# A decoder layer with routed experts: the first layer of half tiles in plain float32, and high and low weights side by side in the second layer

## The chip, the core and the metric

The kernel runs on one core of a Trainium2 chip. Its time is the device time of one execution in microseconds. Five engines work side by side, each through its own list of instructions, and meet at semaphores: TensorE (matrix products, PE in the profile), VectorE (DVE), ScalarE (ACT), GpSimd (POOL) and SyncE (SP), which here does nothing but start transfers. A product has a standing operand, which is loaded first (PEld), and a moving one, whose columns stream past it. Results land in eight banks of 512 float32 columns.

## What is computed

A pre-norm decoder layer on 2048 tokens of width 256: linear attention with 16 heads, a cross attention, and a feed-forward layer in which each token goes to two of eight experts. The change touches only the experts:

```python
probs = softmax(einsum('bnd,ed->bne', xn, Wg))      # two experts are chosen for each token
def body(acc, params):
    w1, b1e, w2, b2e, g = params
    h = gelu(einsum('bnd,df->bnf', xn, w1) + b1e)    # 256 -> 1024
    y = einsum('bnf,fd->bnd', h, w2) + b2e           # 1024 -> 256
    return (acc + g[..., None] * y, None)
```

## The kernel before

**Tiles.** A first part computes the attentions and sorts the tokens by expert. The experts then work on 23 tiles of gathered tokens: 16 full tiles of 256 rows (F) and 7 half tiles of 128 rows (H), in the order `KIND = "FFFFF" + "FFHFFHFHFHFFHFHFHF"`. So the half tiles are 7, 10, 12, 14, 17, 19 and 21. Each tile has its own expert, whose weights (1 MB for each layer) are loaded from memory.

**High and low parts.** A product of the type float32r is rounded, so an operand is split in a high part (ScalarE copies it to float32r) and a low part (VectorE subtracts the high part from the original). Three products, high by high, high by low and low by high, then stand for one exact product. Tile 0 in its first layer (`NL = 1`) and tiles 0 to 2 in their second (`NP = 3`) use plain float32 products instead, one for three.

**A full tile.** The first layer has the weights standing and 256 token columns moving: 48 products (L964, L965, L969). The result has the hidden units on the partitions, so ScalarE's GELU takes the bias for each partition, and its high and low parts stand as operands of the second layer: for each 128 rows 24 products of 256 columns (L1020, L1021, L1022), 8 terms of three.

**A half tile.** Its first layer has the tokens standing and 512 columns of weights moving: 12 products by the helper `three` (L446). The result has tokens on the partitions. So VectorE adds the bias row (`add_bias`, L1995, from `b1r`, 512 KB that a transfer has spread over the partitions), ScalarE applies GELU to it (L1408), and eight transposes (`turn`, L989) bring it into the form of the second layer; the high and low parts are then taken from the banks (L1414, L2000).

**The order.** The lists are written out by hand. For a half tile t TensorE does its first layer, the transposes of the next tile's tokens (L453), and the second layer of tile t-1 with `turn(t)` between its two halves. For the full tile after it, it does the first layer and then the half tile's second. The second layer of a tile thus always runs a tile late. `w1r`, `w1h`, `w1l`, `w2r`, `w2h` and `w2l` have two buffers each, `xf` and `hf` have one, and the second layers write banks 5 and 6 (F) or 7 (H). SyncE starts, for each t in turn, the loads `w1(t+1)`, `w2(t)` and the biases of t (and for half tiles `b1r`). A load that waits holds up all those behind it. `w1(t+1)` waits until the low parts of w1(t-1) are made (L499), which is when its buffer is free.

Of the kernel before, what the change touches and what calls it, by code (L numbers as in the profile page):

```python
# [43 lines left out]
def decoder_layer(nc, x, ctx_in, ctxT, aw, ab, awo, xw, xfc, ff, b1, gb, wg, consts, out):  # L44
# [11 lines left out]
    with ExitStack() as top:  # L56
# [174 lines left out]
        w2h0 = sb("w2h0", [P, 2048], f32r)  # L231
        w2l0 = sb("w2l0", [P, 2048], f32r)
# [5 lines left out]
        w2h1 = sb("w2h1", [P, 2048], f32r)  # L238
        w2l1 = sb("w2l1", [P, 2048], f32r)
# [56 lines left out]
        b1r = sb("b1r", [P, F])  # L296
        w1r, w1h, w1l = [w1r0, w1r1], [w1h0, w1h1], [w1l0, w1l1]
        w2r, w2h, w2l = [w2r0, w2r1], [w2h0, w2h1], [w2l0, w2l1]
# [16 lines left out]
        d_rb = sem("d_rb")  # L315
# [24 lines left out]
        m_w1h, m_w1l, m_w2h, m_w2l, m_xp, m_xf, m_xh, m_xl, m_l1, m_hf, m_hh, m_hl, m_l2, m_ya, m_yb, m_gb, m_gx, m_hb, m_ht = (  # L340
            sem(f"m_{n}") for n in ("w1h", "w1l", "w2h", "w2l", "xp", "xf", "xh", "xl", "l1", "hf", "hh", "hl", "l2", "ya", "yb", "gb", "gx", "hb", "ht"))
# [31 lines left out]

        def parts(t):
            return 2 * (t - NL)

        def halves_of(t):
            return 2 * KIND[:t].count("H")
# [58 lines left out]

        def weigh_on_act(t):
            return t < 4
# [18 lines left out]
        def sync(e):  # L458
# [24 lines left out]
            def load_w1(t):  # L483
# [113 lines left out]
        def tensor(e):  # L597
# [330 lines left out]
            def layer1(t, q):  # L928
# [4 lines left out]
                if q == 0 and t >= NL:  # L933
                    e.wait_ge(m_w1l, parts(t) + 2)
                    e.wait_ge(m_xh, t + 1 - NL)
# [12 lines left out]
                if t >= 2 and KIND[t - 1] == "H":  # L948
                    if q < 2:
                        e.wait_ge(m_hb, halves_of(t - 1) + q + 1)  # L950
                    else:
                        e.wait_ge(m_hl, split(t - 1) + q - 1)
# [3 lines left out]
                for m in range(2):  # L956
# [9 lines left out]
                    if q == 0 and m == 0:  # L966
                        e.wait_ge(m_xl, t + 1 - NL)
# [5 lines left out]
            def layer1_half(t, q):  # L973
                k = t % 2
                if q == 0:
                    e.wait_ge(m_w1l, parts(t) + 2)
                    e.wait_ge(m_xl, t + 1 - NL)
                e.wait_ge(m_hf, 8 * (t - 1) + 2 * q + 2)
                c = slice(q * 512, q * 512 + 512)
                three(e, banks[q][:, :], lambda j: xh[k][:, j, 0:128], lambda j: xl[k][:, j, 0:128],  # L980
                      lambda j: w1h[k][:, :].rearrange("p (j n) -> p j n", j=2)[:, j, c],
                      lambda j: w1l[k][:, :].rearrange("p (j n) -> p j n", j=2)[:, j, c], 2, True).then_inc(m_l1, 2)

            def turn(t):
                h = fl(hf)
                for c in range(2):
                    e.wait_ge(m_hf, 8 * t + 4 * c + 4)
                    for j in range(4):
                        last = e.transpose(banks[2 + c][:, j * 128:j * 128 + 128],  # L989
                                           h[:, c * 512 + j * 128:c * 512 + j * 128 + 128], ident)  # L990
                    last.then_inc(m_ht, 1)

            def layer2(t, i, terms=range(8)):
# [20 lines left out]
                w_low = w2l[k][:, :].rearrange("p (j n) -> p j n", j=8)  # L1014
                for j in terms:
# [65 lines left out]
            for t in range(5, NT):  # L1081
                if KIND[t] == "H":
# [4 lines left out]
                    turn(t)  # L1087
# [29 lines left out]
        def scalar(e):  # L1117
# [228 lines left out]
            def x_affine(t):  # L1346
# [3 lines left out]
                if t > NL:  # L1350
                    e.wait_ge(m_xl, t - NL)
# [20 lines left out]
            def gelu(t, q):  # L1372
# [13 lines left out]
                if q == 0 and t >= 1 and KIND[t - 1] == "H":  # L1386
                    e.wait_ge(m_ht, halves_of(t))
# [22 lines left out]
            def turned_high(t, c):  # L1410
                e.wait_ge(m_ht, halves_of(t) + c + 1)
                if c == 0:
                    e.wait_ge(m_l2, BEFORE[t - 1])
                e.activation(hh[t % 2][:, 4 * c:4 * c + 4, 0:128], banks[2 + c][:, :].rearrange("p (j n) -> p j n", j=4),  # L1414
                             ACT.Copy).then_inc(m_hh, 1)
# [66 lines left out]
            for t in range(5, NT):  # L1482
                if KIND[t] == "H":
# [7 lines left out]
                    turned_high(t, 0)  # L1491
                    turned_high(t, 1)
# [3 lines left out]
                if t + 1 < NT:  # L1496
# [9 lines left out]
                if t == 5 or (KIND[t - 1] == "H" and t + 1 < NT):  # L1506
                    x_affine(t + 1)
                gelu(t, 1)
                if t == NT - 1:
# [1031 lines left out]
```

## Times and profile before

| | |
|---|---|
| median of three runs | 404.87 us (402.98 to 405.08) |
| profiled execution, whole | 402.5 us |
| its span on the core | 400.7 us |
| TensorE busy | 390.9 us, 98% |
| VectorE busy | 340.6 us, 85% |
| ScalarE busy | 307.2 us, 77% |
| GpSimd busy | 238.7 us, 60% |
| TensorE's granted clock | 0.999 of full |

The span is the part of the execution from the first to the last instruction. A product's busy time holds its whole way through the array, and neighbours overlap; so what a product costs in a stream is read from the distance between starts, not from its duration. The same holds, less strongly, of ScalarE and VectorE.

### The profile page before, as it was taken

How to read it: one execution, taken by the hardware profiler on the slowest of the kernel's cores; microseconds unless marked ns; L12 is line 12 of the kernel's file. 1: busy time of each engine (PE TensorE's matmuls, PEld its weight loads, DVE VectorE, ACT ScalarE, POOL GpSimd, SP SyncE). 2: the span in 40 equal slices, each digit the busy share in tenths (PEclk: the TensorE clock that was granted, in tenths of full speed). 3: DMA queues.
4: the chain of work that ended last, by engine and by line, in shares of the span. 5: the costliest groups of instructions: out<-in, count | busy, mean ns of one | idle time of the engine just before them, and what ended most of it. 6: DMA issues, size and time to landing. Idle time of an engine off the chain costs nothing.

```text
span 400.7 us, 8846 instructions
## 1 busy us (share of the span) xinstructions
PE 390.9 (98%) x2953; PEld 372.4 (93%) x2953; DVE 340.6 (85%) x847; ACT 307.2 (77%) x621; POOL 238.7 (60%) x353
## 2 busy tenths in 40 slices
PE   7999999999999999999999999999999999999994
PEld 7789899999989999899999999999999999999994
DVE  5697788888889878899685999979999988999972
ACT  5577777686776769346999988988988988989770
POOL 3546476757667666878873765546656373645443
PEclk9999999999999999999999999999999999999999
DMA  7920031220102742678599798996989897899633
GB/s 256 349 98 29 1 103 48 66 80 27 56 28 65 269 142 96 212 281 265 155 384 295 224 334 262 288 319 216 375 269 345 267 314 266 259 335 315 152 37 39
DMA packets 32738, 79.33 MB, mean 198 GB/s; under 512 B 4691, under 2 KB 24021, under 8 KB 26806
## 3 DMA queue, kind: packets, MB, share of 16 engines
q1 hardware_dynamic: 23728, 67.68, 48.1%
q0 software_dynamic: 7488, 10.39, 12.4%
q10 hardware_dynamic: 1478, 0.72, 0.7%
q8 instruction: 23, 0.38, 0.4%
q14 instruction: 21, 0.17, 0.1%
HBM read 69.14 MB, written 9.63 MB: 197 GB/s over the span
## 4 chain that ended last, share of the span: by engine, by line
PE 91%; DVE 4%; POOL 1%; issue 1%; DMA 1%; ACT 1%; ACTq 0%; DVEq 0%
PE bank L446 21%; PE bank L1020 8%; PE bank L1021 8%; PE bank L1022 8%; PE bank L964 7%; PE bank L969 7%; PE bank L965 7%; PE bank L453 6%; PE bank L1008 3%; PE bank L961 2%; PE bank L816 2%; PE bank L768 2%; PE bank L989 2%; PE bank L683 1%; PE bank L798 1%
## 5 line engine op out<-in xcount | busy, mean ns | idle before, releaser
L2425 POOL DMA_INDIRECT y_<-yb,idxs x29 | 55.3, 1906 | 68.6 <-DMA y_<-yb,idxs 42.3
L1020 PE MATMUL bank<-w2h,hh 128*128 128x256 f32 x264 | 75.4, 286 | 0.0
L1021 PE MATMUL bank<-w2l,hh 128*128 128x256 f32 x264 | 74.1, 281 | 0.0
L1022 PE MATMUL bank<-w2h,hl 128*128 128x256 f32 x264 | 74.1, 281 | 0.0
L964 PE MATMUL bank<-xh,w1h 128*128 128x256 f32 x240 | 64.3, 290 | 0.0
L965 PE MATMUL bank<-xh,w1l 128*128 128x256 f32 x240 | 62.6, 282 | 0.0
L2369 POOL DMA_INDIRECT xg<-xn_rows,idxg x39 | 48.9, 1254 | 15.6 <-issue 11.3
L1702 DVE TENSOR_TENSOR w1l<-w1r,w1h 128x1024 fp32r<-128x1024 f32 x44 | 53.7, 1221 | 2.0 <-ACT w1h L1131 1.7
L1978 DVE TENSOR_TENSOR w2l<-w2r,w2h 128x1024 fp32r<-128x1024 f32 x40 | 48.6, 1218 | 2.5 <-ACT w2h L1138 2.5
L1021 PEld LDWEIGHTS bank<-w2l,hh 128*128 128x128 f32 x264 | 50.0, 189 | 0.0
L1020 PEld LDWEIGHTS bank<-w2h,hh 128*128 128x128 f32 x264 | 50.0, 189 | 0.0
L1022 PEld LDWEIGHTS bank<-w2h,hl 128*128 128x128 f32 x264 | 49.9, 189 | 0.0
L1138 ACT ACTIVATE w2h<-w2r 128x1024 fp32r<-128x1024 f32 x40 | 41.1, 1055 | 10.7 <-PE bank L1022 8.6
L969 PE MATMUL bank<-xl,w1h 128*128 128x256 f32 x240 | 48.3, 283 | 0.0
L1390 ACT ACTIVATE hf<-bank,bs 128x256 f32<-128x256 f32 x104 | 42.1, 477 | 5.5 <-PE bank L969 4.9
L1131 ACT ACTIVATE w1h<-w1r 128x1024 fp32r<-128x1024 f32 x44 | 44.5, 1052 | 2.3 <-DMA w1r<-ff_ 2.3
L965 PEld LDWEIGHTS bank<-xh,w1l 128*128 128x128 f32 x240 | 45.8, 191 | 0.1
L964 PEld LDWEIGHTS bank<-xh,w1h 128*128 128x128 f32 x240 | 45.8, 191 | 0.1
L969 PEld LDWEIGHTS bank<-xl,w1h 128*128 128x128 f32 x240 | 37.3, 191 | 0.0
L1354 ACT ACTIVATE xf<-bank,gbT 128x256 f32<-128x256 f32 (+1 forms) x46 | 21.9, 529 | 12.0 <-PE bank L453 8.3
L2007 DVE TENSOR_TENSOR hl<-hf,hh 128x1024 fp32r<-128x1024 f32 x25 | 30.1, 1223 | 0.6 <-issue 0.6
L2425 POOL DMA_INDIRECT y_<-yb,idxg x10 | 20.5, 2053 | 15.2 <-ACT yb L1370 6.8
(309 smaller groups left out, 1103.3 us busy)
## 6 DMA issues: line engine op xcount, KB each, us to landing
w1r<-ff_ SPq DMA_DIRECT2D x23, 1024.0 KB
w2r<-ff_ SPq DMA_DIRECT2D x23, 1024.0 KB
b1r<-b_ SPq DMA_DIRECT2D x7, 512.0 KB
bs<-ff_ SPq DMA_DIRECT2D x23, 132.0 KB
xn_rows<-xn SPq DMA_DIRECT2D x8, 264.0 KB, 2.2
xin<-x_ SPq DMA_DIRECT2D x8, 256.0 KB, 7.0
cT<-ctxT_ SPq DMA_DIRECT2D x8, 256.0 KB, 4.5
cin<-ctx_ SPq DMA_DIRECT2D x8, 256.0 KB, 3.2
```

The lines of the kernel that those rows point to most:

```text
L446: r = e.matmul(o, a_(t), b_(t), start=first and m == 0, stop=m == n - 1)
L964: e.matmul(o, w_high[:, j, c], xh[k][:, j, :], start=j == 0, stop=False)
L965: e.matmul(o, w_low[:, j, c], xh[k][:, j, :], start=False, stop=False)
L969: last = e.matmul(o, w_high[:, j, c], xl[k][:, j, :], start=False, stop=j == 1)
L1020: e.matmul(bank_y(t, i)[:, 0:D], hh[k][:, j, c], w_high[:, j, :], start=j == 0, stop=False)
L1021: e.matmul(bank_y(t, i)[:, 0:D], hh[k][:, j, c], w_low[:, j, :], start=False, stop=False)
L1022: last = e.matmul(bank_y(t, i)[:, 0:D], hl[k][:, j, c], w_high[:, j, :], start=False, stop=j == 7)
L1131: e.activation(w1h[k][:, s], w1r[k][:, s], ACT.Copy).then_inc(m_w1h, 1)
L1702: e.tensor_tensor(w1l[k][:, s], w1r[k][:, s], w1h[k][:, s].bitcast(fp32), ALU.subtract).then_inc(m_w1l, 1)
L1978: e.tensor_tensor(w2l[k][:, s], w2r[k][:, s], w2h[k][:, s].bitcast(fp32), ALU.subtract).then_inc(m_w2l, 1)
L2369: e.indirect_dma_start(out=xg[k][:, i, :], out_offset=None, in_=xn_d[0:ready, :], in_offset=bass.IndirectOffsetOnAxis(ap=idxg[:, COL[t] + ...
L2425: e.indirect_dma_start(out=out[:, :], out_offset=bass.IndirectOffsetOnAxis(ap=at, axis=0), in_=yb[t % 2][:, i, :], in_offset=None, compute ...
```

## The change

There are two edits. Half tiles: the first layer becomes 16 plain float32 products with the original weights standing and 128 token columns moving; its weights and tokens are no longer split, `add_bias`, `turn` and the load of `b1r` are gone, and GELU takes the bias for each partition in eight operations of 128 columns. Second layers of tiles 3 to 20: high and low weights lie side by side in one tensor `w2s`, so that one product of 512 columns gives high by high in columns 0 to 255 of the bank and high by low in columns 256 to 511; the third product is as before. VectorE then adds the two halves with one operation more for each 128 rows (30 of these).

```diff
@@ load_w1
-                if t >= NL + 2:
+                if t >= NL + 2 and KIND[t - 2] == "F":
                     e.wait_ge(m_w1l, parts(t - 1))
+                if t >= NL + 2 and KIND[t - 2] == "H":
+                    e.wait_ge(m_l1, 4 * (t - 1))
@@ load_b
-                if KIND[t] == "H":
-
-                    if halves_of(t):
-                        e.wait_ge(m_hb, halves_of(t))
-                    else:
-                        e.wait_ge(p_lg, NB)
-                    e.dma_start(b1r[:, :], b1[bass.ds(regs[t], 1), :].to_broadcast([P, F])).then_inc(d_rb, 16)
@@ layer1_half
                 if q == 0:
-                    e.wait_ge(m_w1l, parts(t) + 2)
-                    e.wait_ge(m_xl, t + 1 - NL)
+                    e.wait_ge(d_w1[k], 16 * (t // 2 + 1))
+                    e.wait_ge(m_xf, 2 * t + 2)
                 e.wait_ge(m_hf, 8 * (t - 1) + 2 * q + 2)
-                c = slice(q * 512, q * 512 + 512)
-                three(e, banks[q][:, :], ...).then_inc(m_l1, 2)
-
-            def turn(t):
-                ...
+                w_plain = w1r[k][:, :].rearrange("p (j n) -> p j n", j=2)
+                for m in range(4):
+                    c = slice((4 * q + m) * 128, (4 * q + m + 1) * 128)
+                    for j in range(2):
+                        last = e.matmul(banks[q][:, m * 128:(m + 1) * 128], w_plain[:, j, c], xf[:, j, 0:128],
+                                        start=j == 0, stop=j == 1)
+                last.then_inc(m_l1, 2)
@@ layer2
+                    if side_by_side(t):
+                        if j == 7:
+                            e.matmul(bank_y(t, i)[:, 0:D], hl[k][:, j, c], w_high[:, j, :], start=False, stop=False)
+                        last = e.matmul(bank_y(t, i)[:, :].rearrange("p (s n) -> p s n", s=2), hh[k][:, j, c], w_both[:, :, j, :],
+                                        start=j == 0, stop=j == 7)
+                        if j < 7:
+                            e.matmul(bank_y(t, i)[:, 0:D], hl[k][:, j, c], w_high[:, j, :], start=False, stop=False)
+                        continue
@@ scalar
             def x_affine(t):
-                if t > NL:
-                    e.wait_ge(m_xl, t - NL)
+                if t > NL and KIND[t - 1] == "F":
+                    e.wait_ge(m_xl, splits(t))
+                if t > NL and KIND[t - 1] == "H":
+                    e.wait_ge(m_l1, 4 * t)
@@
             def gelu_half(t, c):
-                e.wait_ge(m_hb, halves_of(t) + c + 1)
-                h = fl(hf)[:, c * 512:c * 512 + 512]
-                e.activation(h, h, ACT.Gelu_apprx_tanh).then_inc(m_hf, 4)
+                e.wait_ge(m_l1, 4 * t + 2 * c + 2)
+                e.wait_ge(m_hl, split(t - 1) + c + 1)
+                ...
+                for m in range(4):
+                    j = 4 * c + m
+                    e.activation(hf[:, j, 0:128], banks[c][:, m * 128:(m + 1) * 128], ACT.Gelu_apprx_tanh,
+                                 bias=bs_[t % 3][:, j:j + 1]).then_inc(m_hf, 1)
@@ the full tile behind a half one: the high parts of the next w1 come after gelu(t, 1)
+                after = KIND[t - 1] == "H" and t + 1 < NT
-                if t + 1 < NT:
+                if not after and t + 1 < NT and KIND[t + 1] == "F":
                     w1_high(t + 1, 0)
                     w1_high(t + 1, 1)
...
                 gelu(t, 1)
+                if after and KIND[t + 1] == "F":
+                    w1_high(t + 1, 0)
+                    w1_high(t + 1, 1)
@@ vector, weigh
+                if side_by_side(t):
+                    e.tensor_tensor(ya[:, i, :], bank_y(t, i)[:, D:2 * D], bs_[t % 3][:, 8:8 + D], ALU.add).then_inc(m_yl, 1)
+                    e.wait_ge(m_yl, n - BEFORE[NP] + 1)
+                    e.tensor_tensor(ya[:, i, :], bank_y(t, i)[:, 0:D], ya[:, i, :], ALU.add).then_inc(m_ya, 1)
```

Here `side_by_side(t)` is `NP <= t < NT - 2`. `add_bias` leaves VectorE's list; its splits of w1 and x are made for full tiles alone; behind a half tile it makes the low parts of w2 before those of the next w1.

On TensorE, at half tile 12, the list before begins its first layer so (`w1h`, `w1l`: high and low weights; `xh`, `xl`: tokens), and further down has the transposes of `turn`:

```order
L446 MATMUL bank<-w1h,xh 128x512 [waits m_hf,m_xl,m_w1l]
L446 MATMUL bank<-w1l,xh 128x512
L446 MATMUL bank<-w1h,xl 128x512
L446 MATMUL bank<-w1h,xh 128x512
```

```order
L989 MATMUL bank<-cs,hf 128x128 [waits m_hf]
L989 MATMUL bank<-cs,hf 128x128 x3
```

The changed list has for both the rows below (`w1r`: the weights as loaded, `xf`: the tokens), and behind them the second layer of the tile before in pairs of a 512 and a 256 column product (`w2s`: both parts of the weights):

```order
L975 MATMUL bank<-xf,w1r 128x128 [waits m_hf,m_xf,d_w11]
L975 MATMUL bank<-xf,w1r 128x128 x7
L975 MATMUL bank<-xf,w1r 128x128 [waits m_hf]
L975 MATMUL bank<-xf,w1r 128x128 x7
```

```order
L1010 MATMUL bank<-w2s,hh 128x512 [waits m_hl,m_ya,m_w2l]
L1013 MATMUL bank<-w2s,hl 128x256
L1010 MATMUL bank<-w2s,hh 128x512
L1013 MATMUL bank<-w2s,hl 128x256
```

The half tile's first layer no longer waits for splits but for the loaded weights and the scaled tokens, and its transposes are gone.

SyncE's list before, for t of a half tile and the full tile behind it (`w1r` and `w2r` are 1 MB loads):

```order
L512 ISA [waits m_hb]
L512 DMA b1r<-b1_ 128x1024
L499 TENSOR_LOAD tei [waits m_w1l]
L499 ISA x2
L500 ISA
L500 DMA w1r0<-ff_ 128x2048
L526 ISA [waits m_w2l]
L526 DMA w2r1<-ff_ 128x2048
```

And changed:

```order
L501 TENSOR_LOAD tei [waits m_l1]
L501 ISA x2
L502 ISA
L502 DMA w1r0<-ff_ 128x2048
L521 ISA [waits m_w2l]
L521 DMA w2r1<-ff_ 128x2048
```

The load of `w1r` for the second tile behind a half tile now waits for the half tile's first layer on TensorE (`m_l1`) and no longer for VectorE's low parts (`m_w1l`), and the `w2r` of the tile between stands behind it.

## Rows read from the trace of the kernel before

**Rows 1.** Page, part 1: busy time, share and instructions of each engine.

```profile
PE 390.9 (98%) x2953; PEld 372.4 (93%) x2953; DVE 340.6 (85%) x847; ACT 307.2 (77%) x621; POOL 238.7 (60%) x353
```

**Rows 2.** Page, part 4: shares of the chain that ended last, by engine.

```profile
PE 91%; DVE 4%; POOL 1%; issue 1%; DMA 1%; ACT 1%; ACTq 0%; DVEq 0%
```

**Rows 3.** Waits of TensorE, the two longest: total us, times, longest.

```profile
PE bank L864 <- POOL xnT L2191: 1.4, 1, 1.4
PE bank L625 <- DVE aw_l L1586: 1.0, 1, 1.0
```

**Rows 4.** Busy time in stretches: half and full tile 12, 13; then 14 to 16.

```profile
core 0: us, PE busy (x) PEld busy (x) DVE busy (x) ACT busy (x) POOL busy (x), PEclk, DMA share, GB/s
...
284.94:303.48 18.54, 18.54 (x148) 18.00 (x147) 18.03 (x29) 16.69 (x26) 11.99 (x7) 1.00 0.95 320
303.48:333.90 30.42, 30.42 (x248) 29.87 (x247) 27.06 (x44) 26.52 (x42) 16.31 (x11) 1.00 0.93 306
```

**Rows 5.** TensorE in time at half tile 12: start us, busy us, operation.

```profile
284.78 0.40 PE L446 MATMUL bank<-w1h,xh 128*128 128x512 f32 x1
...
287.53 0.60 PE L453 MATMUL bank<-cs,xg 128*128 128x128 f32 x4
...
290.80 1.03 PE L989 MATMUL bank<-cs,hf 128*128 128x128 f32 x8
291.59 0.36 PE L1020 MATMUL bank<-w2h,hh 128*128 128x256 f32 x1
291.79 0.28 PE L1021 MATMUL bank<-w2l,hh 128*128 128x256 f32 x1
...
294.50 0.28 PE L964 MATMUL bank<-xh,w1h 128*128 128x256 f32 x1
```

**Rows 6.** TensorE in time at its plain float32 products.

```profile
100.61 1.05 PE L768 MATMUL bank<-va,phk 128*128 128x129 f32 x8
101.50 0.96 PE L683 MATMUL bank<-wg_f,xnT 128*128 128x8 f32 x8
...
150.62 3.62 PE L961 MATMUL bank<-xf,w1r 128*128 128x256 f32 x16
154.07 0.60 PE L453 MATMUL bank<-cs,qsb 128*128 128x128 f32 x4
```

**Rows 7.** VectorE in time at half tile 12.

```profile
286.06 0.41 DVE L2053 TENSOR_TENSOR ya<-bank,bs 128x256 f32<-128x256 f32 x1
286.51 0.35 DVE L2060 TENSOR_SCALAR yb<-ya,small 128x256 f32<-128x256 f32 x1
...
288.34 1.22 DVE L1702 TENSOR_TENSOR w1l<-w1r,w1h 128x1024 fp32r<-128x1024 f32 x1
289.47 1.22 DVE L1978 TENSOR_TENSOR w2l<-w2r,w2h 128x1024 fp32r<-128x1024 f32 x1
```

**Rows 8.** ScalarE in time at tiles 12 and 13; in brackets idle time before and its end.

```profile
285.04 1.06 ACT L1138 ACTIVATE w2h<-w2r 128x1024 fp32r<-128x1024 f32 x1 [0.75 <-PE bank L1022]
286.01 1.99 ACT L1131 ACTIVATE w1h<-w1r 128x1024 fp32r<-128x1024 f32 x2
287.90 1.25 ACT L1408 ACTIVATE hf<-hf 128x512 f32<-128x512 f32 x2
289.05 1.00 ACT L1354 ACTIVATE xf<-bank,gbT 128x256 f32<-128x256 f32 x2
...
297.79 0.81 ACT L1354 ACTIVATE xf<-bank,gbT 128x128 f32<-128x128 f32 x2 [0.30 <-issue]
298.49 1.57 ACT L1390 ACTIVATE hf<-bank,bs 128x256 f32<-128x256 f32 x4
```

**Rows 9.** SyncE in time: the issues of 1 MB loads around half tile 14.

```profile
301.11 0.33 SPq L500 DMA_DIRECT2D w1r<-ff_  x1
302.32 0.33 SPq L526 DMA_DIRECT2D w2r<-ff_  x1
```

**Rows 10.** Transfers from 284 to 304 us in 40 slices: GB/s moved.

```profile
GB/s 473 387 475 410 393 410 361 426 410 442 317 215 272 255 235 206 36 21 0 213 180 344 426 426 410 426 311 229 410 426 336 207 258 425 418 428 448 281 361 369
```

More of the change, by code:

```diff
@@ L41, with decoder_layer @@
 NCONST = _at
-def decoder_layer(nc, x, ctx_in, ctxT, aw, ab, awo, xw, xfc, ff, b1, gb, wg, consts, out):
+def decoder_layer(nc, x, ctx_in, ctxT, aw, ab, awo, xw, xfc, ff, gb, wg, consts, out):
     fp32 = mybir.dt.float32
@@ L295, in decoder_layer @@
         yb1 = sb("yb1", [P, 2, D])
-        b1r = sb("b1r", [P, F])
         w1r, w1h, w1l = [w1r0, w1r1], [w1h0, w1h1], [w1l0, w1l1]
-        w2r, w2h, w2l = [w2r0, w2r1], [w2h0, w2h1], [w2l0, w2l1]
+        w2r, w2s = [w2r0, w2r1], [w2s0, w2s1]
+        w2h, w2l = [w[:, 0, :] for w in w2s], [w[:, 1, :] for w in w2s]
         hp = [hp0, hp1]
@@ L372, in split, with splits @@
             return 2 * (t - NP)
+        def splits(t):
+            return KIND[NL:t].count("F")
         def parts(t):
-            return 2 * (t - NL)
-        def halves_of(t):
-            return 2 * KIND[:t].count("H")
+            return 2 * splits(t)
         def ry(t, name):
@@ L436, in high_on_act, with side_by_side @@
             return t < NE
+        def side_by_side(t):
+            return NP <= t < NT - 2
         def weigh_on_act(t):
@@ L934, in layer1 @@
                     e.wait_ge(m_w1l, parts(t) + 2)
-                    e.wait_ge(m_xh, t + 1 - NL)
+                    e.wait_ge(m_xh, splits(t) + 1)
                 if t == 0 and q == 2:
@@ L947, in layer1 @@
                     e.wait_ge(m_hf, 8 * (t - 1) + 2 * q + 2)
[L948 to L952, printed above, removed]
+                if t >= 2 and KIND[t - 1] == "H" and q < 2:
+                    e.wait_ge(m_hf, 8 * (t - 1) + 4 * q + 4)
                 w_plain = w1r[k][:, :].rearrange("p (j n) -> p j n", j=2)
@@ L966, in layer1 @@
                     if q == 0 and m == 0:
-                        e.wait_ge(m_xl, t + 1 - NL)
+                        e.wait_ge(m_xl, splits(t) + 1)
                     for j in range(2):
@@ L1505, in scalar @@
                     weigh(3, 1)
-                if t == 5 or (KIND[t - 1] == "H" and t + 1 < NT):
+                if t == 5 or after:
                     x_affine(t + 1)
                 gelu(t, 1)
+                if after and KIND[t + 1] == "F":
+                    w1_high(t + 1, 0)
+                    w1_high(t + 1, 1)
                 if t == NT - 1:
@@ L1986, in x_split, with half_low @@
                     e.tensor_copy(xh[k][:, :, 0:n], xf[:, :, 0:n]).then_inc(m_xh, 1)
-                e.wait_ge(m_xh, t + 1 - NL)
+                e.wait_ge(m_xh, splits(t) + 1)
                 e.tensor_tensor(xl[k][:, :, 0:n], xf[:, :, 0:n], xh[k][:, :, 0:n].bitcast(fp32), ALU.subtract).then_inc(m_xl, 1)
-            def add_bias(t, c):
-                e.wait_ge(m_l1, 4 * t + 2 * c + 2)
-                e.wait_ge(d_rb, 8 * halves_of(t) + 16)
-                e.wait_ge(m_hl, split(t) - 1)
-                s = slice(c * 512, c * 512 + 512)
-                e.tensor_tensor(fl(hf)[:, s], banks[c][:, :], b1r[:, s], ALU.add).then_inc(m_hb, 1)
-            def turned_low(t, c):
+            def half_low(t, c):
                 e.wait_ge(m_hh, split(t) + c + 1)
                 s = slice(4 * c, 4 * c + 4)
-                e.tensor_tensor(hl[t % 2][:, s, 0:128], banks[2 + c][:, :].rearrange("p (j n) -> p j n", j=4),
+                e.tensor_tensor(hl[t % 2][:, s, 0:128], hf[:, s, 0:128],
                                 hh[t % 2][:, s, 0:128].bitcast(fp32), ALU.subtract).then_inc(m_hl, 1)
@@ L2052, in weigh @@
                     e.wait_ge(m_yb, BEFORE[t - 1] + i + 1)
-                e.tensor_tensor(ya[:, i, :], bank_y(t, i)[:, 0:D], bs_[t % 3][:, 8:8 + D], ALU.add).then_inc(m_ya, 1)
+                if side_by_side(t):
+                    e.tensor_tensor(ya[:, i, :], bank_y(t, i)[:, D:2 * D], bs_[t % 3][:, 8:8 + D], ALU.add).then_inc(m_yl, 1)
+                    e.wait_ge(m_yl, n - BEFORE[NP] + 1)
+                    e.tensor_tensor(ya[:, i, :], bank_y(t, i)[:, 0:D], ya[:, i, :], ALU.add).then_inc(m_ya, 1)
+                else:
+                    e.tensor_tensor(ya[:, i, :], bank_y(t, i)[:, 0:D], bs_[t % 3][:, 8:8 + D], ALU.add).then_inc(m_ya, 1)
                 if weigh_on_act(t):
@@ L2132, in vector @@
                     w2_low(t, 1)
-                    turned_low(t, 0)
-                    turned_low(t, 1)
+                    half_low(t, 0)
+                    half_low(t, 1)
                     weigh(t - 1, 1)
                 elif KIND[t - 1] == "H":
-                    if t + 1 < NT:
+                    w2_low(t, 0)
+                    w2_low(t, 1)
+                    if t + 1 < NT and KIND[t + 1] == "F":
                         w1_low(t + 1, 0)
-                    w2_low(t, 0)
-                    if t + 1 < NT:
                         w1_low(t + 1, 1)
                         x_split(t + 1)
-                    w2_low(t, 1)
                     if t == NT - 1:
@@ L2155, in vector @@
                 else:
-                    w1_low(t + 1, 0)
-                    x_split(t + 1)
-                    w1_low(t + 1, 1)
+                    if KIND[t + 1] == "F":
+                        w1_low(t + 1, 0)
+                        x_split(t + 1)
+                        w1_low(t + 1, 1)
                     w2_low(t, 0)
```

43 lines of the change are left out of this document (13 added, 30 removed).

## The prediction

> **What bounds the kernel now.** I read the busy times first. TensorE is busy 390.9 of 400.7 us [rows 1]; the others are not near it over the whole span. The chain of work that ended last says the same, 91% of it on TensorE [rows 2], and TensorE's list of waits is almost empty: the two longest are single waits of 1.4 and 1.0 us at the start, far from the experts [rows 3]. In the expert part the reader should see two things in the table by stretch [rows 4]: for a half tile and the full tile behind it (18.54 us) TensorE has no gap, and the others are not far behind: VectorE 18.03, ScalarE 16.69, transfers 0.95 of the time. So time taken from TensorE counts one to one, but only a couple of microseconds for each pair of tiles before something else is late. The working therefore has two steps: what TensorE loses, and whether the others follow.
>
> **Half tiles, first layer.** What goes: 12 products of 512 columns, from 284.78 to 287.53 [rows 5], 2.75 us or 0.229 each, and the eight transposes of `turn`, from 290.80 to the next product at 291.59, plus the 0.08 by which the first product behind them is stretched (0.20 to its successor where 0.12 is normal) [rows 5], 0.87 us. Together 3.62. What comes: 16 plain float32 products with 128 columns moving and new weights each. The nearest row is the plain product of 129 columns, eight from 100.61 to 101.50, 0.111 each [rows 6]; half of a 256 column one would be 0.108 (16 from 150.62 to 154.07 are 0.216 each [rows 6]), and 0.116 would take in some slack. I take 0.111: 1.78 us (1.73 to 1.86). The switch to plain products and back was there before (the transposes of the next tile follow in both), so it costs nothing more. Gain 1.84 us for each half tile, 12.9 us for seven.
>
> The row of the 256 column plain product shows 0.216 us, about two passes of 256 columns at the full clock of 2.4 GHz. The Trainium skill (FP8 and Floating Point Precision, TensorE Precision Notes) says that true float32 takes four passes through the array, which speaks against this edit. By that rule 16 products of 128 columns would be an estimated 16 x 4 x 128 / 2.4 GHz = 3.4 us, and the edit would gain only 0.2 us for each half tile; by the rows it gains 1.84. The measured row contradicts the rule at 256 columns, so I go by the row and keep the rule's outcome as a rival below.
>
> **Second layers.** 30 blocks of 128 rows (12 full tiles of two and 6 half tiles, in tiles 3 to 20), each 24 products of 256 columns. From 291.79 to 294.50 there are 23 of them [rows 5], 0.118 each, so 2.83 us for a block. Now 8 products of 512 and 8 of 256: 8 x (0.229 + 0.118) = 2.78. Gain 0.05 for a block, 1.5 us in all. A joined product saves only the small overhead between two products and one weight load, not columns. Bounds: if a product of 512 ran as tightly as plain ones do (0.216) the gain is 8 x 0.020 = 0.16 for a block, 4.7 us; if joining gave nothing, 0. That the moving operand comes in two strips 8 KB apart isn't shown anywhere in the trace; with 0.006 us for each product, the spread that I see between 512 column ones, it could be a loss of 8 x 30 x 0.006 - 1.5, about nothing. I take 1.5.
>
> So TensorE loses 12.9 + 1.5 = 14.4 us.
>
> **VectorE.** Added: 30 additions like the one at 286.06, 0.45 from start to start [rows 7], 13.5 us. Each is queued ahead of the weighing that writes the rows out, and `ya` is later by 0.45; but the bank is next written a tile later or more, so TensorE doesn't see it. Removed for each half tile: two bias additions of 512 (some 0.6 each by half the 1.13 of 1024 columns [rows 7]), two low parts of w1 (2 x 1.13), one split of x (0.7): about 4.1, for seven 29 us. Taking low parts from `hf` instead of a bank is the same size. Net 15 us lighter. For a pair half + full that is 18.0 - 4.1 + 3 x 0.45 = 15.2, against 16.5 for TensorE. The cover holds.
>
> **ScalarE.** Removed: two high parts of w1 for each half tile, 0.97 each [rows 8], 1.9. GELU: two operations of 512 that took 1.15 [rows 8] become eight of 128. Four of 256 take 1.57 - 0.1, 0.37 each; a 128 column operation is 0.1 shorter than one of 256 (0.81 against 1.00 for a pair of `xf` [rows 8]), so 0.27, and 2.2 for eight (2.9 if a short one costs as much as a long one). Net 16.7 - 1.9 + 1.0 = 15.8 us for a pair, against 16.5. It goes from 90% to 95% of the pair, the tightest of all.
>
> **The load queue.** The new wait is here. Before, w1(16) was issued at 301.11 and w2(15) at 302.32 [rows 9], 2.2 and 1.0 us before half tile 14 began on TensorE (303.32, which is 284.78 [rows 5] and 18.54 for the pair [rows 4]). Now w1 of the second tile behind a half one waits for the half tile's first layer, 1.8 us after it begins, and w2 of the tile between is queued behind it. So both come 3 to 4 us later, as 2.1 MB together. By hand, with 0 at the start of the half tile's first layer and the order of the lists: TensorE does the first layer to 1.8, transposes to 2.2, the second layer of the full tile before to 7.8, the next full tile's first layer with the short transposes to 13.7, and the half tile's second to 16.5. ScalarE, which starts on w2 of the half tile at 0 when its buffer is free, is through w1, GELU, `xf`, w2 and the high parts of h at 8.1, and wants w2 of the full tile then; it would be done at 15.8 of 16.5. `xf` is ready at 6.0, its splits on VectorE at 7.1, and TensorE wants them at 7.8. So that load may be late by some 0.75 + 0.7 = 1.4 us, land at 9.5, 7.7 after its issue, before TensorE waits. Transfers run at 410 to 430 GB/s in bursts [rows 10], 5.1 us for 2.1 MB, or 6.6 at the 320 GB/s of the pair [rows 4]; about 0.9 goes by before the first bytes move. That lands it 6 to 7.5 us after issue: just in time. The bytes themselves fall by 0.5 MB for each half tile (`b1r`).
>
> Where two full tiles follow a half one (tiles 8, 9 and 15, 16) the high parts of the next w1 now stand behind `gelu(t, 1)`, and end at about 15.5 where that load is a microsecond late; low parts and the split of x follow to 17.3 and 17.9, where TensorE wants the high part of x at 17.0: 0.3 to 0.5 us for each. I set 1.5 us for all such waits, with 0 and 6 as ends.
>
> **Sum.** 402.5 (the profiled execution, of which 400.7 is span) - 14.4 + 1.5 = 389.6. The median of the runs shown lay 2.4 above the profiled execution and the lowest 0.5 above; I add 1.4: 391.0 us.
>
> **Rivals.**
> The first: the others don't follow, and ScalarE or the load of w2 takes TensorE's place. For it: 95% load of ScalarE, and a margin of 1.4 us on a load that shares the transfer engines with gathers and scatters. Against: 0.7 us of idle time is left in each pair, and VectorE and the bytes are relieved. If short GELUs cost 0.37, ScalarE needs 16.6 of 16.5 and the chain to `xf` is 0.8 longer; if w2 lands 9 us after issue, 1.3 us are lost. At 0.7 to 1.3 us for each of seven half tiles that is 5 to 9 us: 394.5 to 398.5.
>
> The second: a plain product of 128 columns takes as long as one of 256, 0.216 us [rows 6], because a plain product would be bound by something other than its columns. Then the half tile's layer is 3.46 for 3.62, and the time is 402.5 - 7 x 0.16 - 1.5 + 1.4 = 401.3. Against it: 0.111 at 129 columns and 0.101 at 8 columns in the same trace [rows 6]. The four passes of the page named above would end in the same place.
>
> The third ends slower: w2 behind the held up w1 lands so late that each half tile loses more than the 14.4 / 7 = 2.06 us that it gains. It decides from 7.7 + 2.06 = 9.8 us after issue, 2.1 MB at under 236 GB/s after the first 0.9. Slices of 206 to 235 GB/s exist while scatters run [rows 10], but for 2 us and not for 9. At 200 GB/s the load takes 11.4, each half tile loses 3.7, and the time is 402.5 - 14.4 + 26 + 1.4, about 415; just past the point it is 406.
>
> That the change does nothing: if the pair were in truth bound by transfers (0.95 share [rows 4]), only the bytes saved would count, 0.5 of 5.9 MB, or 1.6 us for each half tile, and the time would be 402.5 - 11 + 1.4 = 393; this lies inside the first rival.
>
> **Chances and range.** Forecast, 388 to 394: 0.72. First rival, with transfers as the bound: 0.18. Second: 0.03. Third: 0.04, nearly all slower. Some smaller mix that ends within half a per cent of before: 0.03. Measured on this kernel, changes under 0.5% can't be told from none. So faster 0.93, same 0.03, slower 0.04. The range goes from 387.0 (the second layers gain 4.7, no waits) to 397.5 (most of the first rival).
>
> **What would show it.** In the changed profile: 16 plain products of a half tile in about 1.8 us with the next transposes right behind; pairs in the second layers at 0.35 us; the pair of tiles 12 and 13 in about 16.6 us and the group of three 14 to 16 in about 28.5 (30.42 before). TensorE's waits should stay under 3 us in the expert part, and be for the splits of x behind a half tile. I am wrong in the step on the load queue if ScalarE's high parts of w2 wait long for transfers, and in the step on TensorE if the 128 column plain products stand further apart than 0.12 us.

## The result: slower by 2.2%, and the profile after

The changed kernel takes 413.51 us (median of four, 410.95 to 415.2) against 404.72 for the kernel before, measured beside it: a ratio of 1.022, 95% interval 1.016 to 1.028. Some executions of either kernel run slower at a slightly lower granted clock, and all times and ratios in this document are of the others. The prediction said 391.0 (387.0 to 397.5) with a chance of 0.93 for faster. It was wrong in size and in sign.

The page of the changed kernel begins its busy times (part 1) and its chain by engine (part 4) so:

```profile
PE 392.7 (95%) x2797; PEld 364.6 (89%) x2797; DVE 325.8 (79%) x835; ACT 299.4 (73%) x649; POOL 240.4 (58%) x353
...
PE 67%; DMA 12%; DVE 10%; ACT 4%; issue 4%; POOL 1%; SPq 1%; ACTq 0%; DVEq 0%; POOLq 0%
```

Against [rows 1, 2]: VectorE and ScalarE are lighter by 15 and 8 us (15 and some 6 were worked out), but TensorE isn't lighter at all (392.7 for 390.9), its share of the span fell, and a quarter of the chain has moved away from it, 11% to transfers and 6% to VectorE. The same stretches as in [rows 4], half and full tile 12 and 13, then 14 to 16:

```profile
core 0: us, PE busy (x) PEld busy (x) DVE busy (x) ACT busy (x) POOL busy (x), PEclk, DMA share, GB/s
...
289.02:307.43 18.41, 18.41 (x136) 17.32 (x135) 15.52 (x25) 15.74 (x31) 11.68 (x8) 1.00 0.88 296
307.43:342.29 34.86, 32.09 (x219) 29.90 (x218) 27.33 (x44) 27.51 (x50) 19.58 (x12) 0.95 0.80 245
```

The pair takes 18.41 for 18.54, where 16.6 was forecast: no gap, so the work itself is not shorter. The group of three takes 34.86 for 30.42, with 2.8 us in which TensorE is idle, and a stretch at a lower clock. Measured from one half tile's first layer to the next, the other group (tiles 7 to 9) went from 30.51 to 33.97, the pair behind tile 19 from 18.62 to 19.74. These, 0.9 us before tile 7 and 1.2 at the end, less 0.6 that the three other pairs gain, are the 10.6 us between the spans (411.3 and 400.7).

**The plain first layer.** TensorE in time at half tile 14, of the changed kernel, and a block of 128 rows in a second layer:

```profile
229.63 0.40 PE L1010 MATMUL bank<-w2s,hh 128*128 128x512 f32 x1
229.87 0.28 PE L1013 MATMUL bank<-w2s,hl 128*128 128x256 f32 x1
229.99 0.39 PE L1010 MATMUL bank<-w2s,hh 128*128 128x512 f32 x1
...
232.43 0.28 PE L956 MATMUL bank<-xh,w1h 128*128 128x256 f32 x1
...
307.43 3.73 PE L975 MATMUL bank<-xf,w1r 128*128 128x128 f32 x32
310.99 0.60 PE L453 MATMUL bank<-cs,xg 128*128 128x128 f32 x4
```

The block takes 2.80 us (229.63 to 232.43; forecast 2.78, before 2.83): that term holds. The first layer takes 3.56 us, not 1.78. The spacing, 0.111, is what was forecast; but there are 32 rows for the 16 products in the code. A plain float32 product stands in the trace as two rows. The same could have been read before, and it holds for the rows at 129 and 8 columns in [rows 6] too: `keys_values` and `crossed_q` have four calls each for their eight rows. The kernel before has 16 plain products in tile 0's first layer (four parts, two blocks, two contraction halves), and its line reads:

```profile
L961 PE MATMUL bank<-xf,w1r 128*128 128x256 f32 x32 | 7.4, 379 | 0.0
```

So the 0.216 of [rows 6] is half a product; a whole one of 256 columns takes 0.43 us, 4 x 256 columns at 2.4 GHz. The rule of the Trainium skill that the prediction set aside (FP8 and Floating Point Precision, TensorE Precision Notes: four passes) agrees with the trace: the estimate by it was 3.4 us for this layer, and 3.56 was measured.

**The groups of three.** SyncE, ScalarE and TensorE of the changed kernel, from half tile 14 (begins at 307.43) to full tile 16:

```profile
311.90 0.33 SPq L502 DMA_DIRECT2D w1r<-ff_  x1
312.42 0.33 SPq L521 DMA_DIRECT2D w2r<-ff_  x1
312.93 0.33 SPq L507 DMA_DIRECT2D bs<-ff_  x1
```

```profile
316.26 1.21 ACT L1414 ACTIVATE hh<-hf 128x512 fp32r<-128x512 f32 x2
321.04 2.01 ACT L1132 ACTIVATE w2s<-w2r 128x1024 fp32r<-128x1024 f32 x2 [3.57 <-DMA w2r<-ff_]
322.95 0.82 ACT L1384 ACTIVATE hf<-bank,bs 128x256 f32<-128x256 f32 x2
323.66 1.02 ACT L1350 ACTIVATE xf<-bank,gbT 128x256 f32<-128x256 f32 x2
324.56 0.85 ACT L1384 ACTIVATE hf<-bank,bs 128x256 f32<-128x256 f32 x2
325.28 2.02 ACT L1125 ACTIVATE w1h<-w1r 128x1024 fp32r<-128x1024 f32 x2
```

```profile
326.04 0.38 PE L453 MATMUL bank<-cs,xg 128*128 128x128 f32 x2
329.19 0.36 PE L956 MATMUL bank<-xh,w1h 128*128 128x256 f32 x1 [2.77 <-DVE w1l L1705]
...
330.46 0.41 PE L956 MATMUL bank<-xh,w1h 128*128 128x256 f32 x1
330.68 0.41 PE L957 MATMUL bank<-xh,w1l 128*128 128x256 f32 x1
```

The loads go out 4.5 us after the half tile begins (1.8 was forecast, the longer first layer is in it). w2 is there 8.6 us after its issue (6 to 7.5 was forecast); ScalarE waits 3.57 us for it. The high parts of w1 (16), whose last packet came at 317.9 and which could have been made in that time, stand behind w2, two GELUs and `xf`; their low parts come at 328.8, and TensorE waits. From 330.4 to 333.0 its products stand 0.21 apart, not 0.12: the granted clock there is 0.50 of full, its lower level (1.2 GHz), and a dozen products cost 1.2 us more. In the chain, 9.84 us are the landing of the biases of tile 15, queued behind both weights:

```profile
312.93 9.84 DMA bs<-ff_
...
325.41 0.96 ACT w1h L1125
326.39 0.98 DVE w1l L1705
327.54 1.23 DVE w1l L1705
```

### The profile page after: what moved, and what is told of

It reads as the page before. It is cut to its first block, busy times and chain, and to the rows that moved or that the text cites. A ratio compares the mean times of both kernels' runs of the same rounds, so it can differ in the third digit from the quotient of the medians.

```text
span 411.3 us, 8487 instructions
## 1 busy us (share of the span) xinstructions
PE 392.7 (95%) x2797; PEld 364.6 (89%) x2797; DVE 325.8 (79%) x835; ACT 299.4 (73%) x649; POOL 240.4 (58%) x353
## 4 chain that ended last, share of the span: by engine, by line
PE 67%; DMA 12%; DVE 10%; ACT 4%; issue 4%; POOL 1%; SPq 1%; ACTq 0%; DVEq 0%; POOLq 0%
PE bank L446 15%; PE bank L1010 7%; DMA bs<-ff_ 7%; PE bank L961 5%; PE bank L956 5%; PE bank L453 5%; PE bank L957 5%; PE bank L975 3%; PE bank L994 3%; PE bank L1013 3%; DMA w2r<-ff_ 2%; DMA y_<-yb,idxs 2%; DVE w1l L1705 2%; PE bank L953 2%; PE bank L811 2%
## 5 line engine op out<-in xcount | busy, mean ns | idle before, releaser
L1010 PE MATMUL bank<-w2s,hh 128*128 128x512 f32 x240 | 86.4, 398 | 0.0
L1132 ACT ACTIVATE w2s<-w2r 128x1024 fp32r<-128x1024 f32 x40 | 41.6, 1068 | 29.4 <-DMA w2r<-ff_ 26.6
L1013 PE MATMUL bank<-w2s,hl 128*128 128x256 f32 x210 | 58.9, 280 | 0.0
L2368 POOL DMA_INDIRECT xg<-xn_rows,idxg x39 | 47.5, 1219 | 16.1 <-issue 10.6
L1981 DVE TENSOR_TENSOR w2s<-w2r,w2s 128x1024 fp32r<-128x1024 f32 x40 | 48.2, 1220 | 10.2 <-ACT w2s L1132 10.2
L1010 PEld LDWEIGHTS bank<-w2s,hh 128*128 128x128 f32 x240 | 44.7, 188 | 8.0
L1384 ACT ACTIVATE hf<-bank,bs 128x256 f32<-128x256 f32 x104 | 42.8, 485 | 10.6 <-PE bank L961 8.8
L1705 DVE TENSOR_TENSOR w1l<-w1r,w1h 128x1024 fp32r<-128x1024 f32 x30 | 36.4, 1221 | 8.4 <-ACT w1h L1125 8.1
L1013 PEld LDWEIGHTS bank<-w2s,hl 128*128 128x128 f32 x210 | 39.6, 188 | 0.3
L1125 ACT ACTIVATE w1h<-w1r 128x1024 fp32r<-128x1024 f32 x30 | 30.5, 1051 | 2.7 <-DMA w1r<-ff_ 2.7
L2424 POOL DMA_INDIRECT y_<-yb,idxg x10 | 19.4, 1940 | 15.8 <-ACT yb L1366 6.4
L1392 ACT ACTIVATE hh<-hf 128x1024 fp32r<-128x1024 f32 x25 | 26.8, 1073 | 0.4
L975 PEld LDWEIGHTS bank<-xf,w1r 128*128 128x128 f32 x224 | 26.0, 192 | 0.4
```

Of the source, the lines that this page charges most:

```text
L1010: last = e.matmul(bank_y(t, i)[:, :].rearrange("p (s n) -> p s n", s=2), hh[k][:, j, c], w_both[:, :, j, :], start=j == 0, stop=j == 7)
L1013: e.matmul(bank_y(t, i)[:, 0:D], hl[k][:, j, c], w_high[:, j, :], start=False, stop=False)
L1132: e.activation(w2h[k][:, s], w2r[k][:, s], ACT.Copy).then_inc(m_w2h, 1)
L1384: e.activation(hidden(t, j), banks[bank1(t, q)][:, m * 256:(m + 1) * 256], ACT.Gelu_apprx_tanh, bias=bs_[t % 3][:, j:j + 1]).then_inc(m_hf, 1)
L1705: e.tensor_tensor(w1l[k][:, s], w1r[k][:, s], w1h[k][:, s].bitcast(fp32), ALU.subtract).then_inc(m_w1l, 1)
L1981: e.tensor_tensor(w2l[k][:, s], w2r[k][:, s], w2h[k][:, s].bitcast(fp32), ALU.subtract).then_inc(m_w2l, 1)
```

## The experiments

Times are medians. Ratios are to the kernel before, measured beside each group of runs, with 95% intervals.

**Each edit alone.** `e1` puts the side by side second layers into the kernel before (its edit is that of the change in `layer2` and `weigh`). `e2` takes them out of the changed one:

```diff
         def side_by_side(t):
-            return NP <= t < NT - 2
+            return False
```

> The kernel before with the side by side second layers alone (tiles 3 to 20); half tiles as before. Theory A (the plain first layer gives TensorE nothing, and the load queue behind it loses the time): this edit is harmless and worth the 1.5 us of overhead in 240 joined products, so about 403.2 us (ratio 0.996), no new waits on TensorE. Theory B (the 30 added additions on VectorE, at 18.0 of 18.5 us in a pair of tiles, delay the low parts): slower than before by 3 us or more, with waits of TensorE for w1l or hl.

> The changed kernel with the three products of before in all second layers and no added additions; so the half tile edit alone. Theory A: the whole loss stays and the 1.5 us of the other edit is missing: 413 to 416 us, TensorE waits for w1l in the two groups half, full, full. Theory B: most of the loss goes, about 404.

e1: 407.88 us, 1.012 (1.004 to 1.020). e2: 409.81 us, 1.013 (1.007 to 1.020). Both edits lose alone. For e1 theory A was wrong and theory B right; the stretches of tiles 10, 11 and of 12, 13 show why:

```profile
core 0: us, PE busy (x) PEld busy (x) DVE busy (x) ACT busy (x) POOL busy (x), PEclk, DMA share, GB/s
265.60:284.50 18.90, 18.90 (x124) 16.79 (x122) 18.59 (x30) 16.57 (x26) 9.80 (x6) 1.00 0.86 265
284.50:304.10 19.60, 19.27 (x124) 16.87 (x123) 19.25 (x32) 16.57 (x26) 9.19 (x6) 1.00 0.93 307
```

VectorE had 18.03 of 18.54 us [rows 4]; three more additions of 0.45 make 19.4, and with 19.25 it is the bound of the second pair. In the changed kernel the half tiles' edit makes room for them (15.52), so the two losses are not to be added: e1's does not occur there. In e2 the pairs are as in the changed kernel (18.49) and the groups about as long (32.63 and 35.48 for 33.97 and 34.86): the loss of the groups belongs to the half tiles' edit.

**The order of the loads, and the cost that was forecast.** `e3` issues w2 and the biases first; `e4` leaves out one contraction half:

```diff
@@ e3
-                if t + 1 < NT:
+                behind = KIND[t - 1] == "H"
+                if t + 1 < NT and not behind:
                     load_w1(t + 1)
                 load_w2(t)
                 load_b(t)
+                if t + 1 < NT and behind:
+                    load_w1(t + 1)
@@ e4, layer1_half
-                    for j in range(2):
+                    for j in range(1):
```

> The changed kernel, but for the full tile behind a half tile SyncE issues w2 and the biases of that tile ahead of w1 of the next tile, so that only this w1 waits for the half tile's first layer. Theory A: ScalarE's wait for w2 (26.6 us in all) goes, so do TensorE's waits of 1.9 and 2.8 us for w1l in the groups half, full, full and the stretch at a low clock behind the second: 402 to 405 us. Rival C (the loss in these groups is made by ScalarE's new order, high parts of w1 behind the second GELU, and not by the loads): still 410 or more.

> The changed kernel with only one of the two contraction halves in the half tiles' plain first layer (8 products for 16, the sum over the other 128 inputs is left out), so that this layer costs TensorE the 1.8 us that was forecast. If the product's cost was the only step that failed, the time falls by 12.5 us below before, to some 391. Theory A (the load queue fails too, whatever the product costs): the loads are issued 1.8 us earlier and are wanted 1.8 us earlier, so the groups half, full, full still lose 3 us each and the pairs begin to lose too: 398 to 403 us.

e3: 406.76 us, 1.004 (1.000 to 1.008); 7 us better than the changed kernel, less than expected. e4: 403.90 us, 1.000 (0.996 to 1.004). In e4 two of the four pairs take the forecast 16.6 us (16.61, 16.55; the others 17.61 and 18.13), but the groups take 35.91 and 34.09, 70.0 us together where the changed kernel has 68.8, though each has 1.8 us less work: TensorE waits 7.0 us for w1l. So the loads fail whatever the product costs. In e3 the wait for w1l is gone, and the first group takes 31.29 us; the second still takes 34.43, with another wait in its place:

```profile
PE bank L453 <- DMA xg<-xn_rows,idxg: 3.6, 4, 2.5
```

These are the gathered tokens of a later tile, which GpSimd issues behind scatters.

**Loads that are never held up.** In `e6` a half tile's w1 goes to its own high or low buffer, unused there, so `w1r` is free as early as before, and that load is issued behind w2 and the biases; w1 is split ahead of w2 again. `e7` is e6 without side by side, `e8` is e6 with one contraction half. `e9` is the kernel before with the new wait added:

```diff
@@ e6, load_w1 (and its own semaphores for half tiles)
-                if t >= NL + 2 and KIND[t - 2] == "F":
+                if t >= NL + 2 and KIND[t] == "F":
                     e.wait_ge(m_w1l, parts(t - 1))
-                if t >= NL + 2 and KIND[t - 2] == "H":
-                    e.wait_ge(m_l1, 4 * (t - 1))
+                if t >= NL + 2 and KIND[t] == "H":
+                    e.wait_ge(m_l1, 4 * (t - 1 if KIND[t - 2] == "F" else t - 3))
@@ e9, load_w1 of the kernel before
+                if t >= NL + 2 and KIND[t - 2] == "H":
+                    e.wait_ge(m_l1, 4 * (t - 1))
```

> The changed kernel (both edits), but a half tile's w1 is loaded into its high or low buffer, which it doesn't use, so that no load waits for a half tile's first layer, and ScalarE and VectorE split the next w1 first, as before. Queue theory: the held up loads are the whole loss, since VectorE is lighter by the half tiles' edit; TensorE then has its 1.5 + 0.35 us back: 401.5 us (ratio 0.995 to 1.0), groups of tiles 7 to 9 and 14 to 16 at 30.2 us. Rival (the longer way to yb and GpSimd's chain of scatters, gathers queued behind them, also loses): 405 or more, with TensorE waiting for gathers.

> As the kernel before in this call, without side by side second layers and their additions. Queue theory: 403, 1.5 us more than with them. Rival: faster than with them, since each weighing is 0.45 us shorter.

> The kernel with free loads and only one of the two contraction halves in the half tiles' plain first layer (the other half of that sum is left out), so the cost that was forecast, 1.8 us, with loads as early as before. If these two steps are all that failed, the time is the forecast's, 388 to 392 us, pairs at 16.6 us and groups of three at 28.4. If ScalarE, transfers or GpSimd's chain can't follow, 393 to 400.

> The kernel before with one wait added: w1 of the second tile behind a half tile is issued only after the half tile's first layer. Nothing else changes. Queue theory: this wait alone costs most of what the change lost, 6 to 10 us, in every pair and group since ScalarE splits w1 first here. Rival (before had 5 us of slack on these loads): no change.

| | us | ratio | 95% |
|---|---|---|---|
| e6 | 404.03 | 1.000 | 0.997 to 1.003 |
| e7 | 404.55 | 1.004 | 1.001 to 1.007 |
| e8 | 404.06 | 1.000 | 0.998 to 1.003 |
| e9 | 404.26 | 1.002 | 1.000 to 1.004 |

e6 brings the time back to that of before. It undoes two things at once, the held up loads and ScalarE's new order, which are taken apart below. It stays above the expected 401.5: its groups take 31.1 us each, and TensorE waits 2.1 us for gathers. e7 is not told apart from it, so no gain or loss of the side by side products is shown here. The same wait in the kernel before costs almost nothing (e9, groups 31.08 and 30.87 for 30.51 and 30.41), which theory had not foreseen. And e8 stayed far from 388 to 392: with the cost of the product and the loads both mended, something else holds it at 404. TensorE's longest waits there are for gathered tokens, and the chain of e8 from 260 to 330 us consists of scatters:

```profile
PE bank L471 <- DMA xg<-xn_rows,idxg: 7.2, 3, 2.9
```

```profile
by line: DMA y_<-yb,idxs 86.7%; POOL y_ L2444 11.2%; issue 9.4%; POOLq L2442 0.2%
...
275.10 2.08 POOL y_ L2444
277.18 0.30 issue
277.49 6.97 DMA y_<-yb,idxs
...
285.25 1.94 POOL y_ L2444
287.19 0.30 issue
287.50 6.93 DMA y_<-yb,idxs
```

GpSimd adds each tile's rows into the output and must not begin before the tile before has landed, since a token can stand in both. A full tile costs two issues and a landing of 7 us, 10 us in all, a half one 7.7: 17.7 us for a pair, where TensorE needs 18.5 in the kernel before and 16.6 here. GpSimd itself is busy 58% of the time.

**Two chains of scatters.** Here odd tiles are added into a second buffer and each scatter waits for the tile two before it:

```diff
-                if t >= 1 and i == 0:
-                    e.wait_ge(d_s, 16 * BEFORE[t])
+                if t >= 2 and i == 0:
+                    e.wait_ge(*scattered(t - 2))
...
-                    out=out[:, :], out_offset=bass...
+                    out=(out_odd if t % 2 else out)[:, :], out_offset=bass...
```

> The kernel before, but tiles take turns between two chains of scatters: odd tiles are added into a second buffer in memory (so their part is missing in the output), and a scatter waits for the landing of the tile two before it, not of the last one. Chain theory (the loop of scatter, landing, next scatter on GpSimd needs as long for a tile as TensorE does, 9.2 us, and is a second bound beside it): TensorE bounds here anyway, so no more than 1 to 3 us less in the expert part, plus some 6 us at the end, where the last scatters no longer wait for each other: 396 to 402. Rival (the chain has slack): only the end changes.

> The changed kernel with the same two chains. If the held up loads alone make its loss in the groups of three, these still take 34 us and the time stays 8 us above the two chain version of before. If the chain of scatters takes part (late yb, gathers late behind it), the groups shrink and the gap too.

> The kernel with free loads and a half tile's first layer at the cost that was forecast (one contraction half left out), with two chains of scatters (odd tiles missing in the output). Chain theory: the chain was what held it at 404; now pairs of tiles take 16.6 us and groups of three 28.5, and the time is 12 to 13 us under the two chain version of before: 384 to 388. Rival (ScalarE or the weights' transfers bound it): within 4 us of it.

> Both edits as they are, with free loads, with two chains of scatters (odd tiles missing in the output). Chain theory: TensorE's saving of 1.5 to 1.9 us shows: that much under the two chain version of before, pairs at 18.4 and groups of three at 30.1 us. Rival: no different from it.

| with two chains | us | ratio | 95% |
|---|---|---|---|
| e10, before | 402.60 | 0.997 | 0.995 to 0.999 |
| e11, changed | 415.34 | 1.027 | 1.019 to 1.036 |
| e12, free loads, forecast cost | 392.61 | 0.970 | 0.964 to 0.977 |
| e13, free loads | 400.93 | 0.992 | 0.989 to 0.995 |

e12 against e8: 11.5 us, so the single chain was what hid the forecast. Its stretches (tiles 12, 13 and 14 to 16), and those of e13:

```profile
280.30:296.90 16.60, 16.60 (x119) 15.54 (x118) 15.45 (x25) 15.18 (x30) 9.60 (x7) 1.00 0.97 311
296.90:326.30 29.40, 29.15 (x204) 26.71 (x203) 26.06 (x43) 25.51 (x47) 18.56 (x11) 1.00 0.88 282
```

```profile
284.20:302.60 18.40, 18.40 (x136) 17.32 (x135) 15.50 (x26) 15.65 (x30) 12.41 (x7) 1.00 0.91 290
302.60:332.70 30.10, 30.10 (x219) 28.32 (x218) 25.61 (x43) 25.15 (x46) 16.87 (x9) 1.00 0.82 255
```

16.60 is the forecast's 16.6, and 392.6 is near its 391.0: the arithmetic on TensorE, VectorE (15.45 for 15.2) and ScalarE (15.18 for 15.8) was sound for a first layer of that cost. The 384 to 388 expected of e12 was too low: it is 10.0 us under e10 and not 12 to 13, its second group takes 29.4 us, and the end did not shorten. e13 against e10 is 1.7 us, TensorE's saving of 1.5 + 0.35. e11 against e13 is 14.4 us, the price of the held up loads together with the new order. The groups of e11 are still 36.19 and 34.15 us, so the chain of scatters did not make the changed kernel's loss; why e11 lies 12.7 us above e10, where 8 was expected, is open. In e10 the end of the run did not shorten by the 6 us that I had expected of it.

**The load or the order.** `e14` is the changed kernel, held up load and all, with w1 split ahead of w2 behind a half tile, as before; `e15` the same with two chains; `e16` is e6 with each gather of tile t + 5 ahead of the scatters of t.

```diff
@@ e14, scalar (VectorE's list likewise)
-                if not after and t + 1 < NT and KIND[t + 1] == "F":
+                if t + 1 < NT and KIND[t + 1] == "F":
                     w1_high(t + 1, 0)
                     w1_high(t + 1, 1)
...
-                if after and KIND[t + 1] == "F":
-                    w1_high(t + 1, 0)
-                    w1_high(t + 1, 1)
@@ e16, gpsimd
+                if t >= 6 and t + 5 < NT:
+                    gather(t + 5)
                 for i in range(ROWS[t]):
                     scatter(t, i)
```

> The changed kernel with its held up load, but behind a half tile ScalarE and VectorE split the next w1 ahead of w2 as before. Theory D (the loss in the groups needs both, the held up load and an order in which w1's high parts stand behind w2, the late load, and two GELUs): groups of three at 31 us in place of 34 and 35, time 405 to 407. Rival (the held up load alone): groups and time as in the changed kernel, 412 or more.

> The same with two chains of scatters (odd tiles missing in the output), so that the chain doesn't blur it. Theory D: 401 to 403, close to the version with free loads (400.9), where the changed kernel with two chains took 415.3. Rival: 412 or more.

> Both edits with free loads, and on GpSimd each gather ahead of the scatters that it was queued behind, so that it is issued while they wait. Theory: TensorE's waits for gathers (2.1 us in the version with free loads) go, the chain of scatters stays as long as it is: 402.5 to 404.5, ratio 0.995 to 1.000. If the chain alone decides, no change from the version with free loads, 405.8.

e14: 404.04 us, 1.000 (0.997 to 1.003). e15: 405.93, 1.004 (1.001 to 1.006). e16: 406.22, 1.004 (1.001 to 1.007). With the old order the changed kernel's loss is gone (1.022 to 1.000), and its two chain version gains 9.4 us: the held up load does its harm through ScalarE's order, as theory D has it. The new order with loads that are free was not run, so what the order costs alone is not shown; e3, which keeps it and frees w2, has 7 us of the loss back. With one chain the held up load costs nothing behind the old order (e14 and e6 are both at 404.0). With two it does: e15 is 5.0 us above e13, where 401 to 403 was expected. Its groups are short (30.78 and 30.19), but two later pairs take 19.06 and 19.75, and there ScalarE waits for w2 and TensorE behind it:

```profile
349.89 2.01 ACT L1138 ACTIVATE w2s<-w2r 128x1024 fp32r<-128x1024 f32 x2 [7.36 <-DMA w2r<-ff_]
```

```profile
353.42 3.81 PE L981 MATMUL bank<-xf,w1r 128*128 128x128 f32 x32 [0.57 <-ACT xf L1356]
...
364.10 0.35 PE L962 MATMUL bank<-xh,w1h 128*128 128x256 f32 x1 [0.76 <-DVE w1l L1708]
```

These two waits are 1.3 of the 5.0 us; the rest is open. e16 did not help: gathers first didn't make the time of e6 shorter, and the cause wasn't followed up. No version that computes the whole layer was faster than the kernel before; one that used TensorE's 1.7 us would probably need a shorter chain of scatters.

## Why the prediction was wrong, point by point

Three steps failed: the cost of the plain first layer (3.56 us and not 1.78), the wait for the loads (3.5 and 4.4 us in the two groups and not 0.3 to 0.5), and the chain of scatters, which the forecast did not have. No single one of the three explains it. With the cost alone mended the time is 403.9 us (e4), with cost and loads 404.1 (e8), with all three 392.6 (e12); with loads and chain mended and the cost as it is, 400.9 (e13). The first took away the gain, the second made the kernel slower, and the third would have hidden the gain had there been one.

- **What bounds the kernel.** TensorE bounds it, that was right (e10: two chains change it by 0.3%). "So time taken from TensorE counts one to one, but only a couple of microseconds for each pair" was too generous: GpSimd's chain takes 17.7 us for a pair (e8) against 18.5. The waits of TensorE can't show it, since it was just in time. It stood in the kernel before in GpSimd's own waits and list:

```profile
POOL y_ L2425 <- DMA y_<-yb,idxs: 42.3, 12, 5.2
POOL y_ L2425 <- DVE yb L2060: 20.1, 6, 6.6
```

```profile
312.82 2.31 POOL L2425 DMA_INDIRECT y_<-yb,idxs  x1 [3.86 <-DVE yb L2060]
...
321.32 2.44 POOL L2425 DMA_INDIRECT y_<-yb,idxs  x1 [4.90 <-DMA y_<-yb,idxs]
324.06 1.55 POOL L2425 DMA_INDIRECT y_<-yb,idxs  x1 [0.30 <-issue]
```

The 42.3 us are waits for its own scatters, and count as used; the 20.1 us of waits for VectorE's rows are the little slack that there was. I named VectorE, ScalarE and transfers, and not this one. It would have cost the forecast 11.5 us (e8, e12).

- **Half tiles, first layer: "16 plain float32 products ... I take 0.111: 1.78 us".** This step took away the gain. Each product is two rows in the trace, and I took a row for a product; it costs 0.22, the layer 3.56, and the edit gains some 0.05 us for a half tile in place of 1.84. The second rival had the right outcome for this term (3.46) and got a chance of 0.03; what spoke against it, the 0.111 and 0.101 at 129 and 8 columns, were half products as well. With free loads and two chains its 401.3 is met (e13: 400.9).

- **Second layers.** 2.80 for a block against 2.78. Right within 0.02 us; with the half tiles' 0.35 it is the 1.7 us of e13. The low end of the range was added up wrongly: with 4.7 us from the second layers and no waits the sum gives 386.3, not 387.0.

- **VectorE and ScalarE.** Loads right (15.52 and 15.74 for 15.2 and 15.8). That the second layers' edit alone makes VectorE the bound (e1) could have been worked out from the same numbers.

- **The load queue: "It lands 6 to 7.5 us after issue: just in time", and 1.5 us for all waits.** Wrong in size: 8.6 us for w2 and 9.8 for the biases behind it, from an issue at 4.5 and not at 1.8. The groups of three were rightly seen as the weak place, with ScalarE's new order as the reason; 0.3 to 0.5 us was the price given, 3.5 and 4.4 the one paid. The time per group also holds the clock's step down after a wait, which was in no term. The third rival (w2 so late that the gain is lost, 406 to 415) got 0.04 and had the right sign and the right engine waiting, but not the mechanism: w2 landed 8.6 us after its issue, short of its 9.8; three of the four pairs lost nothing, while the groups lost most; and it needed the new order on ScalarE, without which the late load costs this kernel nothing (e14). That its 406 to 415 holds the measured 413.5 is luck in part, since it has the full gain of 14.4 us in its sum, which was not there.

## What to carry to other kernels

Before a row of the trace is used as a price, count its instances against the calls in the code: 32 rows for 16 products would have turned this forecast round. When the bound engine is to be relieved, look for loops that include a transfer's landing (scatter, landing, next scatter) and compare their period with that of the bound engine, whatever share of the time the engine that issues them is busy. A load that is made to wait for a late event is not cheap because its own data is needed late: what counts is what stands behind it in its queue, and what stands behind those data on the engine that consumes them.

## What the runs showed of the hardware

- A plain float32 product appears as two rows of half its time: 0.111 us each with 128 columns moving and 0.216 with 256, so 0.22 and 0.43 for a product.
- In the changed kernel TensorE stood idle for 2.8 us and began again at 329.2 us; from 330.4 to 333.0 its granted clock was at the lower level (0.50 of full), and products of 256 columns stood 0.21 us apart for 0.12.
- Scatters that add into memory took mostly 6.3 to 7.9 us to land in e8, one 10.5, in a chain that doesn't overlap itself.
- The same wait of a load cost nothing behind one list order (e9; e14 against e6), 5.0 us behind it with two chains of scatters (e15 against e13), and 14.4 us together with another order on ScalarE (e11 against e13).
